# One maximum instead of a product and a sum per block of edges, one-hots made earlier, and 13 even chunks in two matmul layers

## The chip, the core and the metric

The kernel runs on one core of a Trainium2 chip. The metric is device time in microseconds (us), the median of several runs. Times in the profile are counted from the first instruction of one profiled execution. PE is the matmul engine (TensorE) and PEld its weight load, DVE is VectorE, ACT is ScalarE, POOL is GpSimd, SP is the engine that issues most transfers. PSUM is the memory that matmuls write to: 8 banks of 512 fp32 numbers in each of 128 partitions.

## The reference, cut to what matters

A two-layer graph network on 6250 nodes with 256 features and 106250 edges (`src`, `dst`, a weight each):

```python
edge_index = jnp.stack([src, dst])
h = jnp.maximum(_layernorm(x, axis=-1), 0.0)
x = x + L0(h, weight, hop_logits, src, dst, edge_weight)    # two hops of a weighted gather and sum by src
h = jnp.maximum(_layernorm(x, axis=-1), 0.0)
x = x + L1(h, edge_index, ...)
# L1:
agg = segment_sum(x[src], dst)
h = (1.0 + eps) * x + agg
h = elu(bn(h @ W1 + b1))     # 256 -> 512
h = elu(bn(h @ W2 + b2))     # 512 -> 1024
h = elu(bn(h @ W3 + b3))     # 1024 -> 512
return h @ W4 + b4           # 512 -> 256
```

`bn` takes mean and variance over all 6250 nodes, so no layer can begin before the one before has ended for every node. The edges come sorted by `dst`. The first part sums by `src`, so the kernel sorts the edges again on the chip.

## The kernel before, in words

**Norm and projection (0 to 94 us).** The nodes are worked in 13 chunks: 12 of 512 and one of 106. Each is normalised, turned (PE, L1736), multiplied by the first weight (L1753) and stored as a table of rows (SP, L571). Beside this, DVE makes 32 of 52 one-hots (`make_bins`, L1154). The 832 tiles of 128 edges are cut into 16 bins of 52; one-hot `t` says for tile `t` of each of the 16 bins, and for each of its 128 edges (partitions), in which of 49 windows of 128 nodes the edge's `src` lies: 128 partitions by 16 x 49 = 784 bf16 numbers. The 32 first ones lie in the space of `sum_b`. The other 20 lie in the space of `work`, part of which still holds the rows of the projection on their way out, so DVE makes them only once all the stores (`sup_stored`) have landed.

**Counting (90 to 113 us).** PE sums every one-hot with a matrix of ones, in two halves of 392 columns (8 bins each), 104 matmuls into two banks (L1771). They wait for `bins_made` step by step. `h_cols` of the last chunk, and PE's own projection before them, stand ahead. From the counts DVE and PE work out where each window's block of places begins in each bin (113 to 129 us); these seeds are put into banks 0 and 1 (L1787).

**Rank (129 to 228 us).** For every edge the place among the edges of its bin and window is needed. Banks 0 and 1 (one a half) hold a running count by bin and window. For each of 52 steps `t` and each half, PE adds `before` times one-hot `t` (L1811: to each partition, the number of edges of lower partitions in each window); DVE multiplies the bank by the one-hot itself (L1273, `picked`), which leaves one number per bin, and sums it over the 49 windows (L1277) into `place_f`. Before the next step PE adds `not_before` times one-hot `t` (L1809), so that all 128 edges of the step are counted. PE's next step waits for `rank_picked`, that is for the product of this half; DVE waits for `rank_mm`. In DVE's order of work stand the two products of a step and then its two sums.

**Sort and the three gathers (228 to 3797 us).** `place_f` becomes integers (L1283); matmuls with one-hots move the edges inside each bin (L1826), POOL scatters the bins to memory (L738) and they are read back. Then come two hops of gathering rows (POOL, L771), each summed by matmul (L1859), and the gather for the second part (L816, L1934) with the first matmul layer beside it (chunks of 512, `z1_part`).

**Layers 2 and 3 (3824 to 4403 us).** Both go through chunks of columns (nodes): `over_chunks` calls each step for 12 chunks of 512 (`CN`) and one of 106 (`TAIL`). Every product is three matmuls (L1891 to L1893), because each operand is split in a high and a low part. Layer 2 has 8 x 4 = 32 products a chunk, layer 3 has 4 x 8 = 32: 96 matmuls a chunk in either. In the last chunk PE runs `wide` = 256 columns, of which 106 are used. ACT and DVE make the operands (`elu1`, `elu2`), ACT brings the results out of PSUM (`save_z2`, L1034; `save_z3`), DVE takes the batch statistics (L1590). The result of layer 2 goes to memory (SP, `z2_save`, L644, two halves a chunk) and is read back for layer 3 (`z2_load`, L661); the reading waits for the last store. Layer 4 follows from 4403 us.

The order on each engine is that of the code; engines wait for each other by semaphores alone.

Of the kernel before, what the change touches and what calls it, by code (L numbers as in the profile page):

```python
# [89 lines left out]
FAR = 65536.0  # L90

# [3 lines left out]
assert TAIL <= P and FULL % 2 == 0 and GROUPS % RING == 0 and SPARE >= ROWS  # L95
# [57 lines left out]
def gnn(nc, x, src_t, dst_t, dst_g, w_t, wg, logits, eps, W1, b1, g1, be1, W2, b2, g2, be2,  # L153
        W3, b3, g3, be3, W4, b4, out):
    with ExitStack() as ctx:
# [36 lines left out]
        w1_hi_all, w1_hi_sb, _ = both("w1_hi", K1 * H1)  # L192
# [44 lines left out]
        wg_sb = place(DH * D).rearrange("p (k m) -> p k m", k=DH)  # L237
        at = [8 * CW - D]
# [17 lines left out]

        bin_of = dst_loc
        packed = w_sorted[:, 0:TILES]
        place_f = w1_all[:, 0:TILES]
        picked = w1_hi_all[:, 0:2 * HALF].rearrange("p (h g a) -> p h g a", h=2, a=NT)  # L260
# [163 lines left out]
        ranked = sem("ranked")  # L424
# [118 lines left out]
        def _(sp):  # L543
# [94 lines left out]
            def z2_save(i, q, tiles, first):  # L638
                n = CN if tiles == CT else TAIL
# [13 lines left out]
            def z2_load(i, q, tiles, first):  # L653
                n = CN if tiles == CT else TAIL
# [42 lines left out]
        def _(pool):  # L697
# [30 lines left out]
                               base=E - 1 - t0 * P, pattern=[[-P, GT]], channel_multiplier=-1).then_inc(dst_masked, 1)  # L728

# [115 lines left out]
        def _(act):  # L845
# [179 lines left out]
            def save_z2(i, q, tiles, first):  # L1025
                n = CN if tiles == CT else TAIL
# [10 lines left out]
            def elu1(i, q, tiles, first):  # L1037
                n = CN if tiles == CT else TAIL
                c = 2 * i + q
                for k in range(K2):  # L1040
                    elu_terms(0, z[:, k, bass.ds(c * CN, n)], k, c, n, K2)
# [22 lines left out]
            def elu2(i, q, tiles):  # L1064
                n = CN if tiles == CT else TAIL
# [6 lines left out]
            def save_z3(i, q, tiles):  # L1072
                n = CN if tiles == CT else TAIL
                c = 2 * i + q
                for m in range(K4):
                    act.wait_ge(z_mm[2], K4 * c + m + 1)
                    act.activation(z[:, m, bass.ds(c * CN, n)], ps[:, K4 * q + m, 0:n], ACT.Identity,
                                   bias=bvec[2][:, m:m + 1]).then_inc(z_evac[2], 1)
# [22 lines left out]
        def _(dve):  # L1101
# [86 lines left out]
            dve.wait_ge(zeros_stored, 16 * GT)  # L1188
# [3 lines left out]
            for t in range(OH_A, BT):  # L1192
# [86 lines left out]


            dve.wait_ge(ranked, 2 * BT)
            chain(dve.tensor_copy(place_i, place_f))
# [301 lines left out]
            def column_stats(n, i, q, tiles, slices, of):  # L1584
                width = CN if tiles == CT else TAIL
# [49 lines left out]
            def elu1(i, q, tiles, first):  # L1635
                w = CN if tiles == CT else TAIL
# [20 lines left out]
            def elu2(i, q, tiles, first):  # L1657
                w = CN if tiles == CT else TAIL
# [12 lines left out]
            def stats3(i, q, tiles):  # L1671
                column_stats(2, i, q, tiles, K4, lambda m, c, w: z[:, m, bass.ds(c * CN, w)])
# [57 lines left out]
        def _(pe):  # L1730
# [37 lines left out]
            for t in range(BT):  # L1768
                pe.wait_ge(bins_made, t + 1)
                for half in range(2):  # L1770
                    mm = pe.matmul(bank(6 + half, HALF), ones_h[:, 0:1].to_broadcast([P, P]), bins_of(t, half),  # L1771
                                   start=(t == 0), stop=(t == BT - 1))
                    if t == BT - 1:
# [30 lines left out]

            for t in range(BT):
# [149 lines left out]
            def z2(i, q, tiles, first):  # L1955
                n = CN if tiles == CT else wide
# [21 lines left out]
            def z3(i, q, tiles, first):  # L1978
                n = CN if tiles == CT else wide
# [76 lines left out]
```

## Time and profile before

| what | us |
|---|---|
| median of 3 runs (4511.48 to 4515.73) | 4513.52 |
| the profiled execution, its own time | 4512.35 |
| its span, first to last instruction | 4510.5 |
| norm, projection, one-hots and counting | 0 to 113 |
| seeds | 113 to 129 |
| rank | 129 to 228 |
| sort, gathers and layer 1 | 228 to 3824 |
| layer 2 | 3824 to 4105 |
| layer 3 | 4120 to 4403 |
| layer 4 | 4403 to 4510 |

The page's chain of work that ended last, its list of the costliest groups and its slices show that the gathers hold most of the span. The change does not touch them. A line of a timeline gives the start, the length, the engine, the line of code, what is written from what, how many are merged, and in brackets the idle time of that engine just ahead and what ended it. A line of the table by stretches gives the busy time of each engine in that stretch and, behind the engines, the mean granted clock of TensorE, where 1.00 is 2.4 GHz and 0.50 is 1.2 GHz.

### The profile page before, as it was taken

Reading aid. Unit: us, or ns where it says so; the run is one execution under the profiler, and the core shown is the slowest. Engines: PE = TensorE matmul, PEld = TensorE weight load, DVE = VectorE, ACT = ScalarE, POOL = GpSimd, SP = SyncE. Lnnn points to the kernel's source line nnn. Section 1 sums busy time; section 2 is a strip of 40 time slices with the busy share of each in tenths; the row PEclk is TensorE's granted clock in tenths of the full one; section 3 lists DMA queues with packets and bytes.
Section 4 is the critical chain, followed back from the end, with each engine's and each line's share of the span. In section 5 each row is a group of like instructions: output and inputs, shape, how many; then the busy total and the mean of one; then the engine's idle time right before and its main releaser. Section 6 shows DMA issues by size and latency. Waiting matters only on the chain. (4 is left out here: it accounts for less than half of the span.)

```text
span 4510.5 us, 50631 instructions
## 1 busy us (share of the span) xinstructions
PE 3317.1 (74%) x15857; PEld 2707.2 (60%) x15857; DVE 1936.4 (43%) x4586; ACT 796.7 (18%) x1968; POOL 2678.9 (59%) x2705
## 2 busy tenths in 40 slices
PE   6759677777777767777777774566666665998998
PEld 5158555555555556665665564555555555887887
DVE  7989533333333323333333331222222224556765
ACT  4059300000000000000000000000000001545656
POOL 0068677777777767777777775777777775001000
PEclk9679899999999999999999997788888887999999
DMA  4000133333333343333333334433333333223313
GB/s 140 1 2 6 51 110 109 110 114 109 109 109 113 109 95 109 110 110 113 110 110 109 112 109 115 134 105 104 105 105 104 105 105 89 94 93 127 101 60 114
DMA packets 187133, 443.82 MB, mean 98 GB/s; under 512 B 49102, under 2 KB 96514, under 8 KB 180714
## 3 DMA queue, kind: packets, MB, share of 16 engines
q0 software_dynamic: 126464, 336.63, 26.0%
q1 hardware_dynamic: 60501, 105.26, 6.8%
q8 instruction: 68, 1.11, 0.1%
q14 instruction: 100, 0.81, 0.1%
HBM read 382.22 MB, written 59.49 MB: 98 GB/s over the span
## 5 line engine op out<-in xcount | busy, mean ns | idle before, releaser
L1859 PE MATMUL ps<-work 128*128 128x256 f32 x6912 | 1624.9, 389 | 574.5 <-DMA work<-table_hop,idx 574.5
L771 POOL DMA_INDIRECT work<-table_hop,idx x1728 | 1651.5, 956 | 556.6 <-issue 521.8
L1859 PEld LDWEIGHTS ps<-work 128*128 128x128 f32 x6912 | 1295.6, 192 | 901.9 <-DMA work<-table_hop,idx 486.6
L816 POOL DMA_INDIRECT work<-table_gin,idx x832 | 790.8, 950 | 282.3 <-issue 228.3
L1934 PE MATMUL ps<-work 128*128 128x128 f32 x3328 | 574.0, 344 | 409.1 <-DMA work<-table_gin,idx 378.0
L1934 PEld LDWEIGHTS ps<-work 128*128 128x128 f32 x3328 | 528.5, 250 | 479.0 <-DMA work<-table_gin,idx 314.3
L1399 DVE TENSOR_SCALAR work<-iota,w_hi,edge_buf 128x256 f32<-128x256 bf16 x1728 | 580.8, 408 | 18.7 <-issue 17.5
L1512 DVE TENSOR_TENSOR sum_b<-sum_b,ps 128x256 f32 x104 | 43.9, 422 | 800.3 <-PE ps L1934 800.3
L922 ACT COPY idx<-w 128x8 int32 (+1 forms) x216 | 42.1, 197 | 1947.7 <-PE ps L1859 1907.1
L1411 DVE TENSOR_TENSOR sum_b<-sum_b,ps 128x512 f32 x108 | 74.2, 687 | 718.6 <-PE ps L1859 718.6
L1411 DVE TENSOR_TENSOR big<-big,ps 128x512 f32 x108 | 74.3, 688 | 690.0 <-PE ps L1859 690.0
L1891 PE MATMUL ps<-sum_b_r,work_r 128*128 128x512 f32 (+1 forms) x832 | 323.0, 388 | 33.2 <-DVE sum_b_r L1633 17.7
L1892 PE MATMUL ps<-sum_b_r,work_r 128*128 128x512 f32 (+1 forms) x832 | 322.3, 387 | 0.0
L1893 PE MATMUL ps<-sum_b_r,work_r 128*128 128x512 f32 (+1 forms) x832 | 322.3, 387 | 0.0
L1826 PE MATMUL ps<-work 128*128 128x112 f32 x1664 | 203.6, 281 | 66.1 <-ACT work L901 60.3
L1826 PEld LDWEIGHTS ps<-work 128*128 128x128 f32 x1664 | 194.4, 195 | 75.8 <-issue 75.8
L901 ACT ACTIVATE work<-work,edge_buf 128x56 f32<-128x56 f32 x832 | 200.2, 332 | 183.0 <-DVE work L1313 178.5
L738 POOL DMA_INDIRECT sorted_edges<-work x112 | 196.8, 1758 | 46.5 <-issue 33.2
L803 POOL TENSOR_TENSOR work_r<-work,work_r 128x512 fp32r<-128x512 f32 (+1 forms) x12 | 23.8, 1990 | 329.4 <-DVE work_r L1356 329.4
L1891 PEld LDWEIGHTS ps<-sum_b_r,work_r 128*128 128x128 f32 x832 | 157.4, 189 | 68.8 <-issue 33.5
L969 ACT CAST idx<-edge_buf 128x8 int32 (+1 forms) x104 | 20.2, 198 | 941.8 <-PE ps L1934 941.8
L1892 PEld LDWEIGHTS ps<-sum_b_r,work_r 128*128 128x128 f32 x832 | 157.3, 189 | 34.6
(220 smaller groups left out, 2678.7 us busy)
## 6 DMA issues: line engine op xcount, KB each, us to landing
work<-table_hop,idx POOLq DMA_INDIRECT x1728
z_dram<-sum_b SPq DMA_DIRECT2D x24, 1024.0 KB, 3.9
sum_b<-z_dram SPq DMA_DIRECT2D x24, 1024.0 KB, 5.1
work<-table_gin,idx POOLq DMA_INDIRECT x832
big<-x SPq DMA_DIRECT2D x12, 512.0 KB, 6.0
table_hop<-work SPq DMA_DIRECT2D x12, 512.0 KB, 2.9
table_hop<-sum_b SPq DMA_DIRECT2D x12, 512.0 KB, 3.3
x_dram<-big SPq DMA_DIRECT2D x12, 512.0 KB, 3.4
```

What stands on the lines that cost most here:

```text
L738: pool.indirect_dma_start(sorted_dram, bass.IndirectOffsetOnAxis(to_block[:, g * REG + r:g * REG + r + 1], 0), ev_bin[:, g % 3, r * 2 * SL ...
L771: pool.indirect_dma_start(hop_rows[:, par, t, :], None, table[n], bass.IndirectOffsetOnAxis(idx[:, k % HR, t:t + 1], 0)).then_inc(rows_in[ ...
L816: pool.indirect_dma_start(rows[:, par, t, :], None, table[2], bass.IndirectOffsetOnAxis(idx[:, q, t:t + 1], 0)).then_inc(rows_in[par][half ...
L901: last = act.activation(load[:, k % 2, t, :, 1], hot_slot[:, k % 2, t, :], ACT.Copy, scale=w_all[:, k * BATCH + t:k * BATCH + t + 1])
L1399: last = dve.tensor_scalar(hot[:, k % 2, t, :], iota[:, :], loc_sorted[:, at_], w_sorted[:, at_], ALU.is_equal, ALU.mult)
L1411: dve.tensor_tensor(to, to, ps[:, HWIN * par:HWIN * par + HWIN, 0:D], ALU.add).then_inc(hop_add, 1)
L1826: mm = pe.matmul(bank(4 + g % 2, 2 * BCOLS), hot_part[:, k % 2, t, :], load[:, k % 2, t].rearrange("p w v -> p (w v)"), start=(r == 0 and ...
L1859: mm = pe.matmul(ps[:, HWIN * par + b, 0:D], hot[:, par, t, b * P:(b + 1) * P], hop_rows[:, par, t, :], start=(t == 0), stop=(t == GT - 1))
L1891: pe.matmul(to[:, 0:n], hi, a[:, 0, 0:n], start=start, stop=False)
L1892: pe.matmul(to[:, 0:n], hi, a[:, 1, 0:n], start=False, stop=False)
L1893: return pe.matmul(to[:, 0:n], lo, a[:, 0, 0:n], start=False, stop=stop)
L1934: mm = pe.matmul(ps[:, 2 * par + a, 0:WIN], rows[:, par, t, a * P:(a + 1) * P], onehot[:, par, t, :], start=(t == 0), stop=(t == GT - 1))
```

## The change

Three edits.

*Rank.* `before` gets 8192 (`BIG`) on its diagonal (`before_big`), so that the number in an edge's own window is lifted by 8192 above all others. DVE takes the maximum over the 49 windows straight from PSUM and no product any more; 8192 is taken off where the places become integers. After each step PE takes the lift away again with a third matmul per half, by a diagonal of -8192 (`minus_big`). POOL makes the two new matrices, in three instructions, once the projection has left their space.

*One-hots.* Of the 20 that lie in `work`, 12 lie where nothing is on its way out. They are made straight after the norm; the other 8 (`LATE`, steps 41 to 48) wait for the stores as before. The wait for `zeros_stored` ahead of them is gone. PE sums in the new order (`ORDER`).

*Layers 2 and 3.* 12 chunks of 482 (`ZC`) and one of 466 (`ZT`) in place of 12 of 512 and one of 106 run at 256. Layer 1 and layer 4 keep the old chunks. The memory for the result of layer 2 keeps rows of 512, of which 482 or 466 are now used.

```diff
+BIG = 8192.0
+ZC = 2 * -(-N // (2 * CHUNKS))
+ZT = N - FULL * ZC
...
+        LATE = [OH_A + u for u in range(BT - OH_A) if 3600 < (u + 1) * BINS * NT // 2 and u * BINS * NT // 2 < WG_END]
+        ORDER = [t for t in range(BT) if t not in LATE] + LATE
...
+            pool.wait_ge(sup_mm, CHUNKS)
+            pool.memset(minus_big, -BIG).then_inc(consts_made, 1)
+            pool.wait_ge(consts_made, 14)
+            pool.affine_select(out=before_big, in_=before[:, :], compare_op=ALU.not_equal, fill=BIG, base=0,
+                               pattern=[[-1, P]], channel_multiplier=1).then_inc(consts_made, 1)
+            pool.affine_select(out=minus_big, in_=minus_big, compare_op=ALU.is_equal, fill=0.0, base=0,
+                               pattern=[[-1, P]], channel_multiplier=1).then_inc(consts_made, 1)
...
-            dve.wait_ge(zeros_stored, 16 * GT)
+            for t in ORDER[OH_A:BT - len(LATE)]:
+                make_bins(t)
             dve.wait_ge(sup_mm, CHUNKS)
             for q in range(2):
                 dve.wait_ge(sup_stored[q], 16 * len(range(q, CHUNKS, 2)))
-            for t in range(OH_A, BT):
+            for t in LATE:
                 make_bins(t)
...
                     dve.wait_ge(rank_mm, n + 1)
-                    if t > 0:
-                        dve.wait_ge(ranked, n - 1)
                     of = bank(half, HALF).rearrange("p (g a) -> p g a", a=NT)
-                    dve.tensor_tensor(picked[:, half], of, bins_of_all(t)[:, half * HB:(half + 1) * HB, :],
-                                      ALU.mult).then_inc(rank_picked, 1)
-                for half in range(2):
-                    dve.wait_ge(rank_picked, 2 * t + half + 1)
-                    dve.tensor_reduce(by_step[:, t, half * HB:(half + 1) * HB], picked[:, half], AX_X,
-                                      ALU.add).then_inc(ranked, 1)
+                    dve.tensor_reduce(by_step[:, t, half * HB:(half + 1) * HB], of, AX_X, ALU.max).then_inc(rank_picked, 1)
...
-            chain(dve.tensor_copy(place_i, place_f))
+            chain(dve.tensor_scalar(place_i, place_f, -BIG, None, ALU.add))
...
                     if t > 0:
                         pe.wait_ge(rank_picked, 2 * (t - 1) + half + 1)
-                        pe.matmul(bank(half, HALF), not_before[:, :], bins_of(t - 1, half), start=False, stop=True,
-                                  skip_group_check=True)
-                    pe.matmul(bank(half, HALF), before[:, :], bins_of(t, half), start=False, stop=True,
+                        for part in (not_before[:, :], minus_big):
+                            pe.matmul(bank(half, HALF), part, bins_of(t - 1, half), start=False, stop=True,
+                                      skip_group_check=True)
+                    pe.matmul(bank(half, HALF), before_big, bins_of(t, half), start=False, stop=True,
                               skip_group_check=True).then_inc(rank_mm, 1)
...
             def z2(i, q, tiles, first):
-                n = CN if tiles == CT else wide
+                n = ZC if tiles == CT else ZT
```

The last edit stands in the same form in every step of layers 2 and 3 on SP, ACT, DVE and PE (with `TAIL` for `wide` on the first three).

DVE's order between the norm and the counts, before (`work_h` are the one-hots in `work`, `hw` the last small numbers of the norm's stage, L1201 reads the counts):

```order
L1186 TENSOR_SCALAR hw<-hw 128x2 [waits dve_small]
L1154 TENSOR_TENSOR work_h<-iota,edge_buf 128x784 [waits sup_stored0,sup_mm,sup_stored1,zeros_stored,dve_small]
L1154 TENSOR_TENSOR work_h<-iota,edge_buf 128x784 x19
L1201 TENSOR_TENSOR w_hi<-ps,ident 16x392 [waits counted,bins_made]
L1201 TENSOR_TENSOR w_hi<-ps,ident 16x392
```

The same place of the changed kernel:

```order
L1202 TENSOR_SCALAR hw<-hw 128x2 [waits dve_small]
L1170 TENSOR_TENSOR work_h<-iota,edge_buf 128x784 [waits dve_small]
L1170 TENSOR_TENSOR work_h<-iota,edge_buf 128x784 x11
L1170 TENSOR_TENSOR work_h<-iota,edge_buf 128x784 [waits sup_stored1,sup_stored0,sup_mm]
L1170 TENSOR_TENSOR work_h<-iota,edge_buf 128x784 x7
L1218 TENSOR_TENSOR w_hi<-ps,ident 16x392 [waits counted,bins_made]
L1218 TENSOR_TENSOR w_hi<-ps,ident 16x392
```

Twelve one-hots now stand ahead of the wait for the stores, and eight behind it.

PE's order at the start of the rank stage, before (`sum_b_h` is a one-hot; two rows without a wait are the halves of step 0):

```order
L1794 MATMUL ps<-w,ones 128x400 x2
L1811 MATMUL ps<-sum_b_h,before 128x392 x2
L1809 MATMUL ps<-sum_b_h,not_before 128x392
L1811 MATMUL ps<-sum_b_h,before 128x392
L1809 MATMUL ps<-sum_b_h,not_before 128x392
```

And in the changed kernel (`w_hi_h` is the space that holds `before_big` and `minus_big`):

```order
L1804 MATMUL ps<-w,ones 128x400 x2
L1823 MATMUL ps<-sum_b_h,w_hi_h 128x392 x2
L1821 MATMUL ps<-sum_b_h,not_before 128x392
L1821 MATMUL ps<-sum_b_h,w_hi_h 128x392
L1823 MATMUL ps<-sum_b_h,w_hi_h 128x392
L1821 MATMUL ps<-sum_b_h,not_before 128x392
```

Per half of a step PE has three matmuls of 392 columns where it had two. On DVE, the four instructions of a step (two at L1273, two at L1277) become two (L1288).

## Rows read from the trace of the kernel before

**Rows 1.** Busy time by stage: stretch, length, PE, PEld, DVE, ACT, POOL, clock, DMA.
```profile
129.00:228.00 99.00, 68.24 (x207) 16.99 (x206) 98.22 (x209) 0.00 (x0) 0.00 (x0) 0.66 0.00 1
3824.00:4105.00 281.00, 280.71 (x1248) 229.50 (x1248) 150.31 (x257) 135.90 (x203) 0.00 (x0) 0.99 0.22 91
4120.40:4403.00 282.60, 282.46 (x1248) 228.91 (x1248) 211.44 (x365) 179.21 (x253) 11.70 (x7) 0.99 0.25 84
```

**Rows 2.** Rank: DVE's two lines; least, median and greatest ns, first and last start.
```profile
L1273 DVE TENSOR_TENSOR w_hi<-ps,sum_b_h x64: 551/552/567, 129.7 to 188.5; 128x392 f32<-128x392 f32 x64
L1277 DVE TENSOR_REDUCE w<-w_hi x104: 547/548/552, 130.7 to 227.1; 128x8 f32<-128x392 f32 x104
```

**Rows 3.** Rank: timeline, first steps and one later (start, length, idle before).
```profile
129.13 0.83 PE L1811 MATMUL ps<-sum_b_h,before 128*128 128x392 bf16 x2
129.75 1.04 DVE L1273 TENSOR_TENSOR w_hi<-ps,sum_b_h 128x392 f32<-128x392 f32 x2 [2.48 <-PE ps L1811]
130.37 0.51 PE L1809 MATMUL ps<-sum_b_h,not_before 128*128 128x392 bf16 x1 [0.41 <-DVE w_hi L1273]
130.67 0.53 PE L1811 MATMUL ps<-sum_b_h,before 128*128 128x392 bf16 x1
131.00 0.53 PE L1809 MATMUL ps<-sum_b_h,not_before 128*128 128x392 bf16 x1
...
137.89 0.34 PE L1809 MATMUL ps<-sum_b_h,not_before 128*128 128x392 bf16 x1 [0.39 <-DVE w_hi L1273]
138.07 0.33 PE L1811 MATMUL ps<-sum_b_h,before 128*128 128x392 bf16 x1
```

**Rows 4.** A reduction of DVE that reads PSUM, ahead of the rank stage.
```profile
126.25 0.27 DVE L1256 TENSOR_REDUCE reach<-ps 128x1 f32<-128x108 f32 x1
```

**Rows 5.** Granted clock by stretches: counting, rank, a hop, the start of layer 3.
```profile
105.00:110.00 5.00, 3.03 (x12) 0.68 (x12) 5.00 (x6) 0.00 (x0) 0.00 (x0) 1.00 0.00 0
140.00:145.00 5.00, 2.71 (x12) 0.57 (x10) 5.00 (x12) 0.00 (x0) 0.00 (x0) 1.00 0.02 3
190.00:195.00 5.00, 3.82 (x12) 1.05 (x12) 5.00 (x12) 0.00 (x0) 0.00 (x0) 0.50 0.00 0
1000.00:1050.00 50.00, 37.03 (x161) 29.48 (x160) 17.35 (x46) 0.99 (x5) 37.82 (x41) 1.00 0.39 114
4124.00:4126.00 2.00, 2.00 (x9) 1.63 (x8) 1.97 (x4) 1.44 (x2) 1.10 (x1) 0.91 0.88 242
```

**Rows 6.** Timeline from the end of the norm to the counts.
```profile
83.52 0.23 DVE L1186 TENSOR_SCALAR hw<-hw 128x2 f32<-128x2 f32 x1
90.38 10.78 PE L1771 MATMUL ps<-sum_b_h,ones_h 128*128 128x392 bf16 x64
94.25 17.80 DVE L1154 TENSOR_TENSOR work_h<-iota,edge_buf 128x784 bf16<-128x784 bf16 x20 [10.51 <-DMA table_hop<-work]
113.05 1.03 DVE L1201 TENSOR_TENSOR w_hi<-ps,ident 16x392 f32<-16x392 f32 x2 [1.00 <-PE ps L1771]
```

**Rows 7.** Layer 2: first and last of 39 matmuls in a row of 256 columns.
```profile
4100.26 0.28 PE L1891 MATMUL ps<-sum_b_r,work_r 128*128 128x256 f32 x1
4104.76 0.28 PE L1893 MATMUL ps<-sum_b_r,work_r 128*128 128x256 f32 x1
```

**Rows 8.** Layer 2: ACT's results out of PSUM, by size (busy, mean ns).
```profile
L1034 ACT ACTIVATE sum_b<-ps,bvec 128x512 f32<-128x512 f32 x96 | 63.6, 684 | 126.5 <-PE ps L1893 126.4
L1034 ACT ACTIVATE sum_b<-ps,bvec 128x106 f32<-128x106 f32 x8 | 2.8, 350 | 8.2 <-PE ps L1893 7.4 <-DVE edge_buf L1590 0.8
```

**Rows 9.** Transfers of layer 2's result: count, KB each, median us to landing.
```profile
z_dram<-sum_b SPq DMA_DIRECT2D x24, 1024.0 KB, 3.9
z_dram<-sum_b SPq DMA_DIRECT2D x2, 212.0 KB, 2.5
```

**Rows 10.** Start of layer 3: ACT waits for layer 2's result to come back.
```profile
4113.50 1.28 ACT L1018 ACT_TABLE_LOAD   x1 [4.22 <-DMA sum_b<-z_dram]
```

More of the change, by code:

```diff
@@ L191, in gnn @@
         w4_sb = w1_all[:, :].rearrange("p (k m) -> p k m", k=K4)
-        w1_hi_all, w1_hi_sb, _ = both("w1_hi", K1 * H1)
+        w1_hi_all, w1_hi_sb, w1_hi_h = both("w1_hi", K1 * H1)
         iota = sb("iota", [P, HWIN * P], BF16)
@@ L259, in gnn @@
         place_f = w1_all[:, 0:TILES]
-        picked = w1_hi_all[:, 0:2 * HALF].rearrange("p (h g a) -> p h g a", h=2, a=NT)
+        before_big, minus_big = [w1_hi_h[:, 2 * TILES + a * P:2 * TILES + (a + 1) * P] for a in range(2)]
+        assert 2 * TILES + 2 * P <= 2 * K1 * H1 and 2 * HALF <= TILES
         seeds = w1_hi_all[0:BINS, 0:2 * HALF].rearrange("p (g a) -> p g a", a=NT)
@@ L653, in z2_load @@
             def z2_load(i, q, tiles, first):
-                n = CN if tiles == CT else TAIL
+                n = ZC if tiles == CT else ZT
                 of = z2_dram[bass.ds((2 * i + q) * P, P), :].rearrange("p (k n) -> p k n", k=K3)
@@ L1025, in save_z2 @@
             def save_z2(i, q, tiles, first):
-                n = CN if tiles == CT else TAIL
+                n = ZC if tiles == CT else ZT
                 c = 2 * i + q
@@ L1037, in elu1 @@
             def elu1(i, q, tiles, first):
[L1038 removed]
+                n = ZC if tiles == CT else ZT
                 c = 2 * i + q
                 for k in range(K2):
[L1041 removed]
+                    elu_terms(0, z[:, k, bass.ds(c * ZC, n)], k, c, n, K2)
             elu1(0, 0, CT, True)
@@ L1064, in elu2 @@
             def elu2(i, q, tiles):
-                n = CN if tiles == CT else TAIL
+                n = ZC if tiles == CT else ZT
                 c = 2 * i + q
@@ L1072, in save_z3 @@
             def save_z3(i, q, tiles):
-                n = CN if tiles == CT else TAIL
+                n = ZC if tiles == CT else ZT
                 c = 2 * i + q
@@ L1584, in column_stats @@
             def column_stats(n, i, q, tiles, slices, of):
-                width = CN if tiles == CT else TAIL
+                width = ZC if tiles == CT else ZT
                 c = 2 * i + q
@@ L1635, in elu1 @@
             def elu1(i, q, tiles, first):
-                w = CN if tiles == CT else TAIL
+                w = ZC if tiles == CT else ZT
                 if not first:
@@ L1657, in elu2 @@
             def elu2(i, q, tiles, first):
-                w = CN if tiles == CT else TAIL
+                w = ZC if tiles == CT else ZT
                 c = 2 * i + q
@@ L1767, in _ @@
             pe.wait_ge(h_cols, CHUNKS)
-            for t in range(BT):
-                pe.wait_ge(bins_made, t + 1)
+            for n, t in enumerate(ORDER):
+                pe.wait_ge(bins_made, n + 1)
                 for half in range(2):
                     mm = pe.matmul(bank(6 + half, HALF), ones_h[:, 0:1].to_broadcast([P, P]), bins_of(t, half),
-                                   start=(t == 0), stop=(t == BT - 1))
-                    if t == BT - 1:
+                                   start=(n == 0), stop=(n == BT - 1))
+                    if n == BT - 1:
                         mm.then_inc(counted, 1)
@@ L1955, in z2 @@
             def z2(i, q, tiles, first):
-                n = CN if tiles == CT else wide
+                n = ZC if tiles == CT else ZT
                 c = 2 * i + q
@@ L1978, in z3 @@
             def z3(i, q, tiles, first):
-                n = CN if tiles == CT else wide
+                n = ZC if tiles == CT else ZT
                 c = 2 * i + q
```

12 lines of the change are left out of this document (6 added, 6 removed).

## The prediction

> **What bounds the kernel now.** I read three views: the table by stretches, to see which engine is full in each stage that the change touches; then the timeline of those stages, to see which wait ends last; then single lines for durations. In the rank stage DVE is busy 98.22 of 99 us while PE is busy 68 and at a mean clock of 0.66 [rows 1]: DVE sets the pace. Its two lines run from 129.7 to 227.1 + 0.55 = 227.6 us, 97.9 us for 52 steps or 1.88 us a step, which is four instructions 0.47 us apart [rows 2]. Between norm and counts DVE stands idle 10.5 us for the stores of the projection, then makes 20 one-hots in 17.8 us, and PE ends just after the last one [rows 6]: again DVE's late work sets the end. In layers 2 and 3 PE is busy without a gap, 280.7 of 281.0 and 282.5 of 282.6 us at a clock of 0.99 [rows 1]: PE sets the pace. All three lie on the one path to the end, since every stage needs the whole of the one before; what is saved in each comes off the total, with nothing behind it that is tied to a fixed hour: sort, hops and gathers begin when their inputs are there.
>
> **Rank, what goes.** The two products of a step (L1273) go, 104 instructions, and DVE keeps two reductions: alone 2 x 0.47 = 0.94 us a step. But the reduction now also is what PE waits for, and PE has three matmuls a half. So I follow one half round its loop, at the full clock [rows 3]: reduction 0.55 us; from its end to PE's start 0.07 (129.75 + 0.55 to 130.37); matmuls 0.18 + 0.17 + 0.34 (two starts 0.18 apart, at 137.89 and 138.07, the next by the 0.166 of 64 in a row [rows 6], and the last one's length) = 0.69; from the end of a matmul to DVE's start 0.09 (129.13 + 0.53 to 129.75). Together 1.40 us. In that time both halves must be served: DVE needs 0.94 and PE 6 x 0.166 = 1.00, so both fit, and the halves run half a loop apart. That they do overlap is seen in the old stage: PE starts at 130.37, while DVE's second product lasts until 130.79 [rows 3]. So 52 x 1.40 = 72.8 us. At the half clock matmuls start 0.33 apart (130.67 to 131.00), PE alone needs 6 x 0.33 = 1.98 us, more than one loop (0.55 + 0.07 + 0.30 + 0.33 + 0.53 + 0.09 = 1.87), and a step is 1.98.
>
> Which clock? The old stage swings between the levels: 1.00 in one stretch in which PE was busy 2.71 of 5 us, 0.50 in another with 3.82 of 5 [rows 5]. Waiting much longer than it worked, PE lost the full level; it was slow to get it back at the half one. The new loop has PE working without a stop at the half level, as at the start of layer 3, where PE began at 4120.4 and the stretch 4124 to 4126 has 0.91, so that the clock rose at about 4124.4 [rows 1, 5]. At the full level the new loop leaves PE some tenths of a us idle in 1.40; a hop, with PE busy 37.03 of 50 us, keeps 1.00 throughout [rows 5]. So I take the full clock but for the first 4.0 us: two steps at 1.98 instead of 1.40, 1.1 us. Rank: 72.8 + 1.1 = 73.9, a gain of 24.0 us. Bounds: PE alone at full clock, 1.00 a step, gains 45.9; the half clock throughout, 52 x 1.98 = 103.0, loses 5.1.
>
> *A reduction from PSUM* is priced from two rows: the product, which reads PSUM, takes 552 ns and the reduction, which reads SBUF, 548, for the same 392 numbers [rows 2]; a reduction of 108 numbers from PSUM takes 0.27 us [rows 4], on the same line of about 1 ns a number. So no surcharge. The Trainium skill, page "VectorE: DVE Perf Modes", section "The TRN2 errata — SBUF-src ops pay a fixed extra latency per instruction", has a fixed cost of 120 cycles for VectorE from PSUM against 58 from SBUF; at 0.96 GHz the difference would be 65 ns on each loop, 52 x 0.065 = 3.4 us less gain, an estimate by that page. By that rule the time would be some 4477; the trace shows 4 ns.
>
> The rest of the edit: 8192 is taken off in the pass that made integers anyway, so no instruction is added. POOL's three instructions wait for the last projection, about 90 us, some 30 us ahead of their first use; POOL has nothing else queued until the rank stage is over.
>
> **One-hots.** 12 are made from 83.75 (83.52 + 0.23), at 17.8 / 20 = 0.89 each, until 94.4, in what was idle time; the stores landed at 94.25; 8 more end at 101.5 [rows 6]. Then PE is late: it starts at 90.38, and 64 matmuls took 10.78 us, so 0.166 apart; 104 of them without a stop take 103 x 0.166 + 0.33 = 17.4 us, until 107.8. DVE goes on at about 107.9 in place of 113.05 [rows 6]: 5.1 us. Bounds: nothing, if the extra one-hots slow ACT or the stores (no row shows such a thing for the 32 made before), and 113.05 - 101.5 = 11.5 if PE were no limit. I take 5.1, as PE was dense and at 1.00 there. The wait for `zeros_stored` costs nothing either way, as it ended long before.
>
> **Layers 2 and 3.** Matmuls of 256 columns start 4.50 / 38 = 0.1184 us apart [rows 7]. Of layer 2's 281.0 us the last chunk has 96 x 0.1184 = 11.4; the other 1152 matmuls of 512 columns are 269.6 / 1152 = 0.2340 apart [rows 1, 7]. That is 0.000452 us a column. Of 12 chunks, 30 columns less: 1152 x 30 x 0.000452 = 15.6 us off. The last chunk, 466 for 256: 96 x 210 x 0.000452 = 9.1 us more. Net 6.5 us a layer, 13.0 for both.
>
> Against it, the ends of the layers now hang on a large last chunk. ACT's last result of layer 2 takes 350 ns at 106 and 684 at 512, so about 0.65 at 466: 0.3 later [rows 8]. Its store is 932 KB where it was 212: 2.5 us then, 3.9 for 1024 KB [rows 9], so 3.7, or 1.2 later. This is exposed: the reading back waits for it, ACT waits for the reading, 4.2 us of it [rows 10], and PE for ACT and what follows. At the end of layer 3 ACT's last result is 0.3 later and the statistics after it, of the same widths, by about the same: 0.6. So 13.0 - 0.3 - 1.2 - 0.6 = 10.9. Rows in memory are now cut at 482 of 512, so that each transfer is in more and shorter pieces; no row shows what this costs at these sizes. Inside the layers a store or a load has a chunk's time, over 20 us, against 4; at the border between the layers it could add a us or two, or nothing, or take the 6% shorter load's part back. Bounds of the edit: 13 at best, and a loss of 24 if a matmul of 482 or 466 cost as much as one of 512 (below).
>
> **Sum.** 24.0 + 5.1 + 10.9 = 40.0 us. The profiled execution took 4512.35 (span 4510.5 and 1.85 around it), so 4472.4; the median of the runs is 1.2 above it: 4473.5.
>
> **Rivals.**
> 1. *The clock goes on swinging in the rank stage*, as it does now (0.66 on the mean) [rows 1]. Half the steps at 1.40 and half at 1.98 make 87.9 us, a gain of 10.0, and 4487.5 in all. For it: the loop still makes PE stop once or twice a step. Against: these stops are far shorter than the old ones. The Trainium skill, page "TensorE: Matmul & The Clock Gate", section "A second HAM failure mode: psum-queue depth-cycling", says the same of kernels whose PE idles briefly between groups of matmuls as it goes from bank to bank. By that rule this rival would be the likely one; the old stage agrees, 1.00 and 0.50 [rows 5]; the hop's 1.00 with its pauses does not.
> 2. *The half clock throughout*: 103.0 us, PE bound, a loss of 5.1 there; 10.9 in all, 4502.6. Against it: PE without a stop got the full clock at the start of layer 3.
> 3. *A matmul of 482 or 466 columns costs what one of 512 costs*: each layer loses 96 x (0.2340 - 0.1184) = 11.1, with the 2.1 at the ends 24.3 in all, against 29.1 from the first two edits: 4508.7, no change. Against it: halving the columns halves the time [rows 1, 7].
> 4. *The halves of the rank loop do not overlap any more* (the slower side). If PE, which takes its work in order, and DVE, which also does, fell into step so that each half waits for the other, a step would be two loops, 2.80 us, 145.6 in all: 47.7 lost, 31.7 with the rest, 4545. It decides from 2.19 us a step on ((97.9 + 16.0) / 52). Against it: each half has its own bank and its own waits, and the old loop overlaps.
>
> **Chances.** Forecast 0.68, with a range of its own of 4463 to 4483 (a loop between 1.25 and 1.55 us, the layers 4 us up or down); swinging clock 0.17; half clock 0.06; dear matmuls 0.05; no overlap 0.04. The range, 4455 to 4494, takes in the first and the second and most of the way to the bound of 1.00 us a step (4451.6). A measurement of this kernel can tell about 0.2% (9 us) from no change. Faster by more than that: 0.68 + 0.17 + most of 0.06 = 0.90; within it 0.06; slower 0.04.
>
> **What would show it.** In the changed profile: DVE's reductions 104 in number, and from the first to the last 72 to 76 us; both halves' reductions in each 1.40 us, with DVE idle some 0.4 of it and PE named as what ends the wait; the clock near 1.00 there after the first 4 us. DVE's first read of the counts near 108, with PE dense from 90 on. Matmuls 0.220 us apart at 482 columns in layers 2 and 3, those layers 6 us shorter each, and the gap between them about 1.5 us longer. Wrong would be: a step far from 1.40 (the loop or the clock misjudged), a reduction much over 0.55 us, or layers that keep their length.

## The result, and the profile after

The changed kernel takes 4485.02 us (median of 4 runs, 4483.58 to 4485.62) against 4514.62 for the kernel before: a ratio of 0.9933, 95% interval [0.9918, 0.9948], or 30 us less (23 to 37). The forecast was 4473.5: the direction and the range hold, and some 10 us of the gain are missing. The time lies 2 us above the forecast's own narrower range (4463 to 4483) and nearer to the first rival's 4487.5 than to 4473.5, so it takes the trace to tell the two apart. The profiled execution took 4485.46, its span 4483.8 (before: 4512.35 and 4510.5).

In the changed kernel L1288 is the maximum, L1821 and L1823 the rank's matmuls, L1170 the one-hots, L1218 the read of the counts, L1903 to L1905 the matmuls of layers 2 and 3, L754, L787 and L832 GpSimd's scatters, hop gathers and GIN gathers, which are those for the second part (before: L738, L771, L816).

The table by stretches, for the rank stage, then its slow start and the rest, then layers 2 and 3:

```profile
122.60:194.20 71.60, 68.44 (x309) 22.76 (x308) 58.98 (x104) 0.00 (x0) 0.00 (x0) 0.95 0.00 1
122.60:128.80 6.20, 5.80 (x19) 2.21 (x19) 3.31 (x6) 0.00 (x0) 0.00 (x0) 0.50 0.00 0
128.80:194.20 65.40, 62.64 (x292) 20.55 (x290) 55.67 (x98) 0.00 (x0) 0.00 (x0) 1.00 0.00 1
3805.00:4081.20 276.20, 275.56 (x1248) 235.54 (x1248) 149.67 (x256) 136.21 (x204) 0.00 (x0) 0.99 0.25 90
4097.80:4375.10 277.30, 276.48 (x1248) 235.73 (x1248) 211.47 (x366) 179.43 (x254) 11.48 (x7) 0.99 0.27 86
```

Against [rows 1] DVE is no longer full in the rank stage (58.98 of 71.6 us in place of 98.22 of 99), the clock there is 0.50 for the first 6 us and then 1.00, and PE's time in the two layers is 5.2 and 6.0 us shorter. DVE's one line (least, median, greatest ns, first and last start):

```profile
L1288 DVE TENSOR_REDUCE w<-ps x104: 556/568/569, 123.3 to 193.6; 128x8 f32<-128x392 f32 x104
```

And from the timeline of PE one step and the start of the next:

```profile
134.27 0.34 PE L1821 MATMUL ps<-sum_b_h,not_before 128*128 128x392 bf16 x1
134.44 0.33 PE L1821 MATMUL ps<-sum_b_h,w_hi_h 128*128 128x392 bf16 x1
134.61 0.33 PE L1823 MATMUL ps<-sum_b_h,w_hi_h 128*128 128x392 bf16 x1
134.98 0.34 PE L1821 MATMUL ps<-sum_b_h,not_before 128*128 128x392 bf16 x1
135.16 0.33 PE L1821 MATMUL ps<-sum_b_h,w_hi_h 128*128 128x392 bf16 x1
135.32 0.33 PE L1823 MATMUL ps<-sum_b_h,w_hi_h 128*128 128x392 bf16 x1
135.60 0.34 PE L1821 MATMUL ps<-sum_b_h,not_before 128*128 128x392 bf16 x1
```

From 123.3 to 193.6 + 0.57 are 70.9 us, against the 97.9 that the prediction read from [rows 2]. One half comes round from 134.27 to 135.60, 1.33 us, with the other half's matmuls in between. From norm to counts (start, length, idle before):

```profile
82.67 0.23 DVE L1202 TENSOR_SCALAR hw<-hw 128x2 f32<-128x2 f32 x1
82.93 17.80 DVE L1170 TENSOR_TENSOR work_h<-iota,edge_buf 128x784 bf16<-128x784 bf16 x20
89.53 10.78 PE L1781 MATMUL ps<-sum_b_h,ones_h 128*128 128x392 bf16 x64
100.14 6.80 PE L1781 MATMUL ps<-work_h,ones_h 128*128 128x392 bf16 x40
107.05 1.03 DVE L1218 TENSOR_TENSOR w_hi<-ps,ident 16x392 f32<-16x392 f32 x2 [6.32 <-PE ps L1781]
```

The read of the counts stands 24.38 us behind the norm's last instruction, in place of 29.53 [rows 6]: 5.15 us less, and it is now PE that ends last. The border of layers 2 and 3, by ACT's two table loads, and then the stores of layer 2's result (count, KB each, median us to landing):

```profile
4081.40 1.28 ACT L1025 ACT_TABLE_LOAD   x1
4091.01 1.28 ACT L1034 ACT_TABLE_LOAD   x1 [5.41 <-DMA sum_b<-z_dram]
```

```profile
z_dram<-sum_b SPq DMA_DIRECT2D x24, 964.0 KB, 4.1
z_dram<-sum_b SPq DMA_DIRECT2D x2, 932.0 KB, 3.9
```

Before, these table loads stood at 4105.44 and 4113.50 [rows 10 for the second], 8.06 us apart; now 9.61. The wait for the reading back is 5.41 in place of 4.22, and the last store lands in 3.9 us in place of 2.5 [rows 9].

Where the missing gain went is seen in a line that the change doesn't touch, GpSimd's hop gathers; the kernel before, then the changed one (least, median and greatest ns, first and last start), each with its scatters, which come ahead of the gathers:

```profile
L771 POOL DMA_INDIRECT work<-table_hop,idx x1728: 942/946/2000, 518.0 to 2712.2; - x192
L738 POOL DMA_INDIRECT sorted_edges<-work x112: 954/1352/47822, 272.2 to 504.1; - x112
```

```profile
L787 POOL DMA_INDIRECT work<-table_hop,idx x1728: 949/954/2013, 485.4 to 2690.5; - x192
L754 POOL DMA_INDIRECT sorted_edges<-work x112: 963/1353/47865, 239.1 to 471.5; - x112
```

The first gather is 32.6 us earlier, the last one 21.7. Each takes 7 to 8 ns more, in the least and in the median, 1728 times; from first to last they take 2205.1 us in place of 2194.2. The pages have the same lines with their busy time, mean length and idle time, before and after:

```profile
L771 POOL DMA_INDIRECT work<-table_hop,idx x1728 | 1651.5, 956 | 556.6 <-issue 521.8
L787 POOL DMA_INDIRECT work<-table_hop,idx x1728 | 1662.3, 962 | 556.7 <-issue 522.7
```

GpSimd is busy 10.8 us longer and waits as long as before: the hops are longer because the gathers themselves are. The account, from the two traces:

| part | forecast | measured, us gained |
|---|---|---|
| rank, first to last DVE instruction | 24.0 | 27.0 |
| one-hots, norm to counts | 5.1 | 5.15 |
| layers 2 and 3 with border and end | 10.9 | 8.6 |
| hop gathers, first to last | 0 | -10.9 |
| what is left of the span (start, sort, between stages, layer 4) | 0 | -3.1 |
| sum, span | 40.0 | 26.7 |

The last part is not shown to be a cost of the change. Its two largest pieces differ as much among the other twelve kernels: layer 4, from the last table load to the end, is 103.6 us before and 104.7 after, in the others 103.5 to 105.0, with old chunks and new; from the last hop gather to the first GIN gather are 25.7 us before and 27.4 after, in the others 25.1 to 27.5.

### The profile page after: what moved, and what is told of

Its sections match the earlier page's. It is cut to its first block and busy times, and to the rows that moved or that the text cites. A ratio compares the mean times of both kernels' runs of the same rounds, so it can differ in the third digit from the quotient of the medians.

```text
span 4483.8 us, 50632 instructions
## 1 busy us (share of the span) xinstructions
PE 3297.6 (74%) x15959; PEld 2720.9 (61%) x15959; DVE 1898.1 (42%) x4482; ACT 796.5 (18%) x1968; POOL 2702.0 (60%) x2708
## 5 line engine op out<-in xcount | busy, mean ns | idle before, releaser
L787 POOL DMA_INDIRECT work<-table_hop,idx x1728 | 1662.3, 962 | 556.7 <-issue 522.7
L832 POOL DMA_INDIRECT work<-table_gin,idx x832 | 791.5, 951 | 283.9 <-issue 228.8
L1903 PE MATMUL ps<-sum_b_r,work_r 128*128 128x482 f32 (+1 forms) x832 | 318.9, 383 | 35.2 <-DVE sum_b_r L1643 17.9
L1904 PE MATMUL ps<-sum_b_r,work_r 128*128 128x482 f32 (+1 forms) x832 | 318.3, 383 | 0.0
L1905 PE MATMUL ps<-sum_b_r,work_r 128*128 128x482 f32 (+1 forms) x832 | 318.1, 382 | 0.0
L754 POOL DMA_INDIRECT sorted_edges<-work x112 | 197.4, 1762 | 46.8 <-issue 33.2
L819 POOL TENSOR_TENSOR work_r<-work,work_r 128x512 fp32r<-128x512 f32 (+1 forms) x12 | 23.5, 1971 | 326.0 <-DVE work_r L1366 326.0
L1903 PEld LDWEIGHTS ps<-sum_b_r,work_r 128*128 128x128 f32 x832 | 157.3, 189 | 63.0 <-issue 35.6
L1509 DVE TENSOR_SCALAR work<-iota,edge_buf 128x128 f32<-128x128 bf16 x832 | 176.2, 299 | 2.0 <-ACT sum_b L944 2.0
```

What stands on the lines that cost most here:

```text
L754: pool.indirect_dma_start(sorted_dram, bass.IndirectOffsetOnAxis(to_block[:, g * REG + r:g * REG + r + 1], 0), ev_bin[:, g % 3, r * 2 * SL ...
L787: pool.indirect_dma_start(hop_rows[:, par, t, :], None, table[n], bass.IndirectOffsetOnAxis(idx[:, k % HR, t:t + 1], 0)).then_inc(rows_in[ ...
L832: pool.indirect_dma_start(rows[:, par, t, :], None, table[2], bass.IndirectOffsetOnAxis(idx[:, q, t:t + 1], 0)).then_inc(rows_in[par][half ...
L1509: last = dve.tensor_scalar(onehot[:, q % 2, t, :], iota[:, 0:WIN], dst_loc[:, bass.ds(g * GT + t, 1)], None, ALU.is_equal)
L1903: pe.matmul(to[:, 0:n], hi, a[:, 0, 0:n], start=start, stop=False)
L1904: pe.matmul(to[:, 0:n], hi, a[:, 1, 0:n], start=False, stop=False)
```

## The experiments

Three sets of four kernels, each timed beside the kernel before. The kernel before has 4512.65, 4516.10 and 4517.48 us in the three sets, so sets are compared by the ratio to it; the changed kernel's own is to 4514.62. "Hops" is the time from the first to the last start of a hop gather.

| kernel | us | ratio to before, interval | gather, least/median ns | hops, us |
|---|---|---|---|---|
| before | | | 942/946 | 2194.2 |
| changed | 4485.02 | 0.9933 [0.9918, 0.9948] | 949/954 | 2205.1 |
| only_rank | 4497.15 | 0.9964 [0.9950, 0.9978] | 949/953 | 2203.8 |
| only_hot | 4508.37 | 0.9992 [0.9983, 1.0001] | 942/946 | 2193.7 |
| only_chunk | 4505.81 | 0.9984 [0.9975, 0.9993] | 942/946 | 2194.0 |
| dve_big | 4472.90 | 0.9912 [0.9897, 0.9927] | 942/946 | 2192.7 |
| after_tt | 4477.02 | 0.9915 [0.9902, 0.9929] | 942/946 | 2196.3 |
| pool_m3 | 4476.38 | 0.9912 [0.9897, 0.9927] | 942/946 | 2192.7 |
| pool_s1 | 4475.36 | 0.9909 [0.9894, 0.9924] | 942/946 | 2196.4 |
| pool_f3 | 4473.18 | 0.9903 [0.9888, 0.9919] | 942/946 | 2196.1 |
| after_ne | 4479.06 | 0.9914 [0.9898, 0.9931] | 942/947 | 2197.3 |
| after_swap | 4485.79 | 0.9927 [0.9910, 0.9943] | 949/953 | 2207.0 |
| pool_eq1 | 4485.21 | 0.9931 [0.9915, 0.9948] | 949/953 | 2204.0 |
| four_mm | 4485.91 | 0.9927 [0.9911, 0.9944] | 942/946 | 2196.0 |

With short gathers the hops take 2192.7 to 2197.3 us, with long ones 2203.8 to 2207.0. So the 10.9 us of the account is one difference of a spread: the means of the two groups are 10.0 apart.

### Each edit alone, and the matrices made elsewhere

The first set asks which edit carries the longer gathers. *only_rank*, *only_hot* and *only_chunk* are the kernel before with one of the three edits. *dve_big* is the changed kernel without GpSimd's three instructions; DVE makes the matrices behind its last one-hot:

```diff
+            dve.tensor_scalar(minus_big, ident[:, :], -BIG, None, ALU.mult).then_inc(consts_made, 1)
+            dve.scalar_tensor_tensor(out=before_big, in0=ident[:, :], scalar=BIG, in1=before[:, :], op0=ALU.mult,
+                                     op1=ALU.add).then_inc(consts_made, 1)
```

> The kernel before with the new rank alone (three matmuls and one maximum a half, GpSimd's three instructions, no other edit). Both theories: the rank loop is 27 us shorter than before, as in the changed kernel (first maximum to last 70.9 us). Theory A (the three instructions ahead of them make each of GpSimd's 1728 hop gathers some 7 ns longer): median gather 954 ns, the two hops give back about 11 us, time about 16 us under the kernel before (some 4498 us). Theory B (the longer gather comes of the earlier one-hots or of the chunks' other widths, or is one of chip and execution): median gather 946 ns, time about 27 us under the kernel before (some 4487 us).

> The kernel before with the 20 one-hots made without a break alone; GpSimd's program is that of the kernel before. Theory A: gathers at 946 ns, and the whole gain of some 5 to 6 us (DVE's read of the counts at about 107 us in place of 113.05) reaches the end: some 4509 us. Theory B in its form that the one-hots' order moves the gathers: 954 ns, 11 us given back, some 4520 us.

> The kernel before with the even chunks of MLP 2 and 3 alone; GpSimd's program is that of the kernel before. From the two traces layer 2 gains 4.8 us, layer 3 some 5.7 us, the border between them loses 1.5 us and layer 4 another 1.5 us: about 7.5 us under the kernel before, some 4507 us, where the forecast had 10.9 us. Theory A: gathers at 946 ns. Theory B in its form that the chunks' edit moves the gathers: 954 ns and some 4518 us.

> The changed kernel with the two matrices (the lifted triangle and minus 8192 on the diagonal) made by two DVE instructions behind the last one-hot, where DVE waits 6.3 us for the counts, in place of GpSimd's three. Theory A: GpSimd's gathers are back at 946 ns, the hops take as long as before, and the time is about 11 us under the changed kernel's: some 4474 us. Theory B (not of GpSimd's instructions): gathers at 954 ns, some 4485 us. In both the rank loop and the one-hots take what they take in the changed kernel.

All four came out as theory A has it: gathers at 953 ns in only_rank, 946 in the other three. Edit by edit, only_rank gained 15.5 us where its rank loop gives 27, only_hot 4.3 and only_chunk 6.8, each against 4512.65. In only_chunk the table loads of layer 2 and 3 repeat the changed kernel's border:

```profile
4101.58 1.28 ACT L1013 ACT_TABLE_LOAD   x1
4111.44 1.28 ACT L1022 ACT_TABLE_LOAD   x1 [5.65 <-DMA sum_b<-z_dram]
```

9.86 us in place of 8.06. dve_big gained 39.8 us (33 to 46 by its interval), where the forecast had 40.0. Its two new DVE instructions (0.22 and 0.28 us) lie where DVE then still waits 5.98 us for PE:

```profile
102.11 0.22 DVE L1202 TENSOR_SCALAR w_hi_h<-ident 128x128 bf16<-128x128 f32 x1
102.25 0.28 DVE L1203 SCALAR_TENSOR_TENSOR w_hi_h<-ident,before 128x128 bf16<-128x128 f32 x1
108.51 1.02 DVE L1212 TENSOR_TENSOR w_hi<-ps,ident 16x392 f32<-16x392 f32 x2 [5.98 <-PE ps L1775]
```

So GpSimd's three instructions cause it. Whether by their place, their number or their kind was open.

### Place and number, or a state

The gathers are longer from the first to the last, in straight code and in loops, so it is not likely that a loop's code merely lies in another place. A line of the changed kernel's GIN stage says more. GpSimd gathers eight tiles there, makes one subtraction (L819) and gathers on; the gathers ahead of it, the eight behind it, and the eight ahead of it in the kernel before:

```profile
L832 POOL DMA_INDIRECT work<-table_gin,idx x8: 949/954/963, 2717.9 to 2726.7; - x8
L832 POOL DMA_INDIRECT work<-table_gin,idx x8: 946/947/963, 2729.1 to 2737.9; - x8
L816 POOL DMA_INDIRECT work<-table_gin,idx x8: 944/946/1056, 2737.9 to 2746.8; - x8
```

Hence theory K, a state of GpSimd that a subtraction ends. *after_tt* adds one to the changed kernel; the other three add to dve_big, at the place of the three instructions and behind the same wait, something else into unused space:

```diff
+            pool.tensor_tensor(spare, ones[:, 0:64], ones[:, 64:128], ALU.subtract).then_inc(consts_made, 1)
```

*pool_m3* has three fills (one of them shown), *pool_s1* one select from bf16 with `not_equal`, and *pool_f3* three of these, 32 columns each, from the f32 matrix `ones`:

```diff
+            pool.memset(spare[:, 0:32], 0.0).then_inc(consts_made, 1)
```

```diff
+            pool.affine_select(out=spare[:, 0:128], in_=before[:, 0:128], compare_op=ALU.not_equal, fill=0.0, base=0,
+                               pattern=[[-1, 128 - 0]], channel_multiplier=1).then_inc(consts_made, 1)
```

> The changed kernel with one more GpSimd instruction behind its three: a subtraction of two 128x64 constants into unused space. In the changed kernel's trace the first eight gathers of the GIN stage, ahead of GpSimd's first subtraction there, have a median of 954 ns and those behind it 947. Theory K (the three instructions leave GpSimd in a state in which its indirect DMA instructions take 7 to 9 ns longer, and a subtraction ends it): scatters back from a shortest of 963 ns to 954, hop gathers from 954 to 946, time some 11 us under the changed kernel's (4474 us). Theory N (it is the place or the number of GpSimd's instructions, so that one more changes it by chance at most): gathers at 954 ns or another value than 946, some 4485 us.

> The kernel with the two matrices on DVE, and in GpSimd's program, at the place where the changed kernel has its three instructions and behind the same wait, three fills of 128x32 bf16 into unused space. Theory N (place or number): gathers at 954 ns and the time of the changed kernel, some 4484 us. Theory K (the kind of instruction, the select): 946 ns and the time of the kernel with the matrices on DVE, 4473 us.

> The kernel with the two matrices on DVE, and in GpSimd's program at that place one select alone, of 128x128 bf16 from bf16 as the changed kernel's, into unused space. Theory K in the form that the select from bf16 does it: gathers at 954 ns, some 4484 us. Theory N (three instructions' shift): one instruction moves the rest by another length, so 954 ns is not looked for; 946 ns and 4473 us.

> The kernel with the two matrices on DVE, and in GpSimd's program at that place three selects of 128x32 bf16 from f32, the form that the kernel before makes its triangles with. Theory N: gathers at 954 ns, some 4484 us. Theory K in the form that any select does it, when it is GpSimd's last computing instruction but the fills: 954 ns; in the form that it needs a bf16 input: 946 ns, 4473 us. The kernel before has a select of 128x8 f32 as its last one and gathers at 946 ns, which speaks for the latter.

after_tt, with all three instructions still there; its timeline of GpSimd, and its line of hop gathers:

```profile
91.99 10.78 POOL L741 TENSOR_SCALAR_AFFINE_SELECT w_hi_h<-before 128x128 bf16<-128x128 bf16 x1
102.72 0.29 POOL L743 TENSOR_SCALAR_AFFINE_SELECT w_hi_h<-w_hi_h 128x128 bf16<-128x128 bf16 x1
102.99 0.31 POOL L746 TENSOR_TENSOR w_hi<-ones 128x64 f32<-128x64 f32 x1
```

```profile
L789 POOL DMA_INDIRECT work<-table_hop,idx x1728: 942/946/1987, 486.8 to 2683.1; - x192
```

One subtraction of 0.31 us gives the gathers their 946 ns back: the ratio falls from 0.9933 to 0.9915. Theory N fell three times: three instructions more move GpSimd's program without effect (pool_m3, pool_f3), and a fourth takes the effect away. But my form of K fell too: neither a select from bf16 (pool_s1) nor three selects (pool_f3) leave the state. What was left of the changed kernel's instructions and not in these runs: the select that compares with `is_equal`, which nothing else uses, or the sequence of a fill and two selects.

### Which instruction leaves the state

*after_swap* exchanges the changed kernel's two selects, *pool_eq1* is pool_s1 with another comparison, and *after_ne* makes the diagonal matrix the other way round:

```diff
-            pool.memset(minus_big, -BIG).then_inc(consts_made, 1)
+            pool.memset(minus_big, 0.0).then_inc(consts_made, 1)
...
-            pool.affine_select(out=minus_big, in_=minus_big, compare_op=ALU.is_equal, fill=0.0, base=0,
+            pool.affine_select(out=minus_big, in_=minus_big, compare_op=ALU.not_equal, fill=-BIG, base=0,
```

And pool_eq1 against pool_s1:

```diff
-            pool.affine_select(out=spare[:, 0:128], in_=before[:, 0:128], compare_op=ALU.not_equal, fill=0.0, base=0,
+            pool.affine_select(out=spare, in_=before[:, :], compare_op=ALU.is_equal, fill=0.0, base=0,
```

> The changed kernel with its three GpSimd instructions in number, order and place, but the diagonal matrix made the other way round: filled with zero and then minus 8192 put on the diagonal by a select with not_equal, in place of filled with minus 8192 and the rest zeroed by a select with is_equal. Theory E (the select with is_equal, which nothing else in these kernels uses, leaves the state): scatters from 954 ns, hop gathers at 946 ns, some 4475 us. Theory Q (the sequence of a fill and two selects from bf16, or a select in place on bf16, whatever it compares): 963 and 954 ns, some 4485 us.

> The changed kernel with its two selects in the other order, so that the select with is_equal comes first and the one with not_equal last. If the state is that of GpSimd's last select: 946 ns and some 4475 us. If the select with is_equal leaves it and only a subtraction ends it: 954 ns and some 4485 us. Theory Q: 954 ns too.

> The kernel with the two matrices on DVE, and in GpSimd's program one select with is_equal of 128x128 bf16 from bf16 into unused space; the run with one select with not_equal at that place had gathers at 946 ns. Theory E: 954 ns and some 4484 us. Theory Q: 946 ns and some 4474 us.

One word of one instruction decides; what else differs in the two texts names the same 128 columns in another way. pool_s1 with `not_equal`, then pool_eq1 with `is_equal`:

```profile
L783 POOL DMA_INDIRECT work<-table_hop,idx x1728: 942/946/1996, 485.3 to 2681.7; - x192
```

```profile
L783 POOL DMA_INDIRECT work<-table_hop,idx x1728: 949/953/1987, 485.7 to 2689.7; - x192
```

And after_ne, the changed kernel with number, order and place kept:

```profile
L787 POOL DMA_INDIRECT work<-table_hop,idx x1728: 942/947/1962, 486.8 to 2684.1; - x192
```

Theory E holds in all three. after_swap shows that a later select with `not_equal` does not end the state (953 ns), and all four kernels with 953 or 954 ns show that GpSimd's fill of `hop1_sum` (10.55 us long, ahead of the scatters) does not either. The times of this set agree with the traces: the four runs of after_ne (4476.45 to 4480.47) all lie below the eight of after_swap and pool_eq1 (4481.88 to 4491.57). What in GpSimd the state is, stays open: the runs show what leaves it and one instruction that ends it.

### What sets a step of the rank loop

*four_mm* is dve_big with a fourth matmul a half, by a matrix of zeros that DVE makes:

```diff
-                        for part in (not_before[:, :], minus_big):
+                        for part in (not_before[:, :], minus_big, nothing):
```

> The kernel with the two matrices on DVE, and in each half of a step of the rank loop a fourth matmul by a matrix of zeros (52 steps; the matmuls follow each other at 0.167 us). Theory chain (a step is one half's way through PE and then DVE: three matmuls, the maximum, and the two handovers between them, 1.333 us; the other half lies beside it): a step takes 1.50 us, the loop some 8.7 us longer, time some 4482 us. Theory DVE (two maxima of 0.568 us and what lies between them set the step): no change, 4473 us. Theory PE (PE's own matmuls set it, 6 to 8 of them at 0.167 us, 1.00 to 1.33 us): a step of 1.33 us, no change.

DVE's line of maxima in four_mm, and PE's timeline (x2 are two in a row):

```profile
L1284 DVE TENSOR_REDUCE w<-ps x104: 556/567/569, 125.5 to 203.9; 128x8 f32<-128x392 f32 x104
```

```profile
149.75 0.34 PE L1818 MATMUL ps<-sum_b_h,not_before 128*128 128x392 bf16 x1
149.92 0.49 PE L1818 MATMUL ps<-sum_b_h,w_hi_h 128*128 128x392 bf16 x2
150.25 0.33 PE L1820 MATMUL ps<-sum_b_h,w_hi_h 128*128 128x392 bf16 x1
150.57 0.34 PE L1818 MATMUL ps<-sum_b_h,not_before 128*128 128x392 bf16 x1
150.75 0.49 PE L1818 MATMUL ps<-sum_b_h,w_hi_h 128*128 128x392 bf16 x2
151.08 0.33 PE L1820 MATMUL ps<-sum_b_h,w_hi_h 128*128 128x392 bf16 x1
151.25 0.34 PE L1818 MATMUL ps<-sum_b_h,not_before 128*128 128x392 bf16 x1
```

The same half starts at 149.75 and 151.25: 1.50 us a step, as the chain theory has it. From first to last maximum are 78.4 us against 70.3 in dve_big, 8.1 more; the ratio of 0.9927 to 0.9912 is some 7 us. Neither DVE alone (two maxima of 0.567) nor PE alone (eight matmuls at 0.167, 1.33) sets the step.

## Why the prediction was right, and the step that failed

**Rank: the mechanism right, the gain forecast 3.0 us too small.** Following one half round its loop gave 1.40 us; it is 1.33. The matmuls have the forecast's length (134.27 to 134.61 + 0.33 = 0.67, forecast 0.69). The reduction is 0.568, not 0.55. So the two handovers together are 1.33 - 0.67 - 0.57 = 0.09 us, where 0.07 and 0.09 were taken from [rows 3]: that is the term that was too large. The slow start is the smaller miss the other way: the clock came up some 6.5 us into the stage, at 129.1, not after 4.0, and cost 70.9 - 52 x 1.333 = 1.6 us, not 1.1.

**Its rivals.** The swinging clock, the half clock and the halves in step all fell: the mean clock is 1.00 from 128.8 to 194.2, with PE busy 62.64 of 65.4 us. Where PE waits for DVE its matmuls start 0.37 apart (134.61 to 134.98) in place of 0.17. The rule of the Trainium skill, page "TensorE: Matmul & The Clock Gate", section "A second HAM failure mode: psum-queue depth-cycling", has the clock swing when PE idles briefly between groups; this loop's trace does not agree. The old stage's mean was 0.66 [rows 1], and PE there stood idle 0.39 us ahead of a step's first matmul [rows 3] where now it is some 0.04 (134.61 + 0.33 to 134.98). The prediction's reading that PE was "waiting much longer than it worked" when it lost the full level there is not what [rows 5] show, with PE busy 2.71 of 5 us at 1.00; why the old stage's clock fell stays open.

**The reduction from PSUM** takes 568 ns where the one from SBUF took 548 [rows 2]. "So no surcharge" was wrong by 20 ns, 1.0 us over 52 loops, if the change from a sum to a maximum costs nothing, which no run separates. The estimate of 65 ns worked out from the Trainium skill, page "VectorE: DVE Perf Modes", section "The TRN2 errata — SBUF-src ops pay a fixed extra latency per instruction", is three times what is measured.

**One-hots: right in size and cause.** 5.15 us for 5.1, with PE dense to the end. only_hot's 4.3 has an interval of -0.5 to 7.7 us, so the traces show this gain and the times alone do not.

**Layers 2 and 3: right in kind, 2.3 us short.** PE's time fell by 5.15 and 5.98 us where 6.5 each was forecast. The term that was too large is the 15.6 us of 1152 shorter matmuls. At a clock of 1.00 the kernel before and the changed kernel have, over a long stretch of layer 2:

```profile
3830.00:4080.00 250.00, 250.00 (x1077) 202.67 (x1076) 138.45 (x234) 124.53 (x185) 0.00 (x0) 1.00 0.23 93
```

```profile
3815.00:4050.00 235.00, 235.00 (x1070) 200.49 (x1069) 132.25 (x227) 119.19 (x181) 0.00 (x0) 1.00 0.26 93
```

250 / 1077 = 0.2321 and 235 / 1070 = 0.2196, so 1152 x 0.0125 = 14.4. The forecast's 0.2340 was a mean over the layer with its slow start, but that is the smaller part: with 0.2321 the same working gives 0.000444 us a column and 15.3 us. The rest is the price itself, 0.0125 / 30 = 0.00042 us a column between 512 and 482; why it is lower there is open. The costs at the ends were nearly right: ACT's last result 0.65 for 0.35 [rows 8], the border between the table loads +1.55 (1.19 of it in the wait for the reading back, forecast 1.2; the other 0.4 was not forecast), the end of layer 3 +0.37 from table load to table load and +0.3 for ACT's result (forecast 0.6). The shorter rows in memory add little: the store of 964 KB takes 4.1 us, of 1024 KB it took 3.9 [rows 9]. Rival 3, dear matmuls, fell by the same rows.

**The step that failed** is the one on POOL: "POOL's three instructions wait for the last projection, about 90 us, some 30 us ahead of their first use; POOL has nothing else queued until the rank stage is over", a cost of nothing. They did cost nothing where they stand: the matrices were ready at 101.13 and first used at 122.6. But one of them left GpSimd slower at the work that comes after, 7 to 8 ns on each of 1728 hop gathers, and these lie on the path to the end: 10.9 us. The same assumption stands in "sort, hops and gathers begin when their inputs are there": they did begin earlier, by 32.6 us, and did not keep their length. With that one instruction written otherwise (after_ne) the gain is 38.4 us, and with the matrices made by DVE (dve_big) 39.8, against the forecast's 40.0. That this comes so close is in part luck: the rank stage gained 3.0 us more than forecast and the two layers 2.3 less.

**A better version.** dve_big, 4472.9 us (0.9912 of the kernel before), or after_ne with 0.9914, beat the changed kernel (0.9933). Their intervals overlap its own, and they were not timed in one set with it; but the six kernels with all three edits and gathers at 946 or 947 ns (four_mm with its longer loop left aside) have 0.9903 to 0.9915, the three with 953 or 954 0.9927 to 0.9933, and the traces show where the difference lies.

## What to carry to other kernels

Compare, between two profiles, also the least and median duration of the long repeated lines that the change does not touch: 7 to 8 ns on 1728 instructions was a quarter of the gain that was forecast, and no wait or idle time showed it. An instruction that is off the critical path is free only if what its engine does afterwards keeps its length. Where two engines pass a buffer to and fro, follow one buffer round its loop, compare that with each engine's own work, and take spacings from a stretch at one clock, not from a stage's mean.

## What was not expected of the hardware

A GpSimd select of 128 by 128 with `is_equal` left GpSimd's indirect DMA instructions longer: scatters from a least of 954 ns to 963, gathers from 942 to 949, until GpSimd's next tensor subtraction. Selects with `not_equal` and fills neither caused nor ended it. It is not tied to the delay told of next: in only_rank the select with `is_equal` ran undelayed (0.29 us) and left the longer gathers, in pool_s1 a select with `not_equal` was delayed (11.45 us) and left the gathers at 946 ns.

A GpSimd select did not end before DVE's one-hots did. In the changed kernel it runs from 90.10 for 10.78 us, to 100.88, and DVE's 20 one-hots end at 100.73; in only_rank, where DVE waits for the stores until 94.62, the same select takes 0.29:

```profile
90.10 10.78 POOL L741 TENSOR_SCALAR_AFFINE_SELECT w_hi_h<-before 128x128 bf16<-128x128 bf16 x1
```

```profile
91.31 0.29 POOL L738 TENSOR_SCALAR_AFFINE_SELECT w_hi_h<-before 128x128 bf16<-128x128 bf16 x1
```

Three fills, which read nothing, took 0.12 us each at that place while DVE made one-hots (pool_m3).

The Trainium skill, page "GPSIMD Engine Reference", section "1. Specifications", says that GpSimd's way to SBUF is shared with VectorE and that instructions of VectorE with two SBUF inputs contend for it; the one-hots have two, and the trace agrees. It cost nothing here, with 21 us between 101.13 and the first use.
